# Two convolution-attention blocks on one core: the begin rebuilt, batch norm and block 1's weights prepared later

## The reference

```python
x = x + L0(gn(x)); x = x + L1(gn(x))

def L0(f):                      # linear attention, 8 heads of 16
    x = chan_ln(f, g_norm)      # over channels, at each position
    q, k, v = (depthwise3x3(w1 @ x, dw) for each of the three)
    q = softmax(q, channels of a head) * 16**-0.5;  k = softmax(k, positions)
    ctx = k v^T  per head;  out = silu(q ctx)
    return chan_ln(out_w @ out, g_out)

def L1(x):                      # ReLU linear attention, heads of 8
    qkv = w_qkv @ x
    y = grouped1x1(depthwise5x5(qkv, w_dw), w_pw)
    m = concat(qkv, y); q, k = relu, relu; v gets a row of ones
    out = (v k^T) q, divided by its last row
    return batchnorm(w_proj @ out)   # with given mean and variance
```

## Time and profile before

| | us |
|---|---|
| median of 3 runs (314.0 to 317.98) | 317.24 |
| the profiled execution | 313.73 |
| its span, first to last instruction | 312.0 |
| busy in it: PE, DVE, ACT, POOL | 252.5, 196.5, 150.9, 109.8 |

### The profile page before, as it was taken

How to read it: one execution, slowest core, us unless ns; L and a number is a source line. 1 busy time by engine, 2 the same in 40 slices (tenths; PEclk the granted TensorE clock), 3 DMA queues, 4 the chain that set the end, 5 groups by cost and what they waited for, 6 DMA issues and landing times. The chain is left out here.

```text
span 312.0 us, 13310 instructions
## 1 busy us (share of the span) xinstructions
PE 252.5 (81%) x5715; PEld 190.7 (61%) x5715; DVE 196.5 (63%) x640; ACT 150.9 (48%) x364; POOL 109.8 (35%) x311
## 2 busy tenths in 40 slices
PE   0347799739889599975789979978999989889995
PEld 0235577517568477764566757766877767567761
DVE  3788887408987457999697875654324233457674
ACT  0457575318983467665453537531433347522220
POOL 8035555006866417763341314111112111253200
PEclk9999799959999999999599999999999999999999
DMA  7720078990001200000008281753000000002112
GB/s 235 123 47 3 0 171 211 213 218 9 4 4 24 45 3 2 2 2 0 3 2 184 44 183 41 169 143 65 4 4 4 4 4 4 2 4 69 69 47 91
DMA packets 15499, 19.18 MB, mean 61 GB/s; under 512 B 3904, under 2 KB 9024, under 8 KB 15440
## 3 DMA queue, kind: packets, MB, share of 16 engines
q1 hardware_dynamic: 11936, 17.15, 22.8%
q10 hardware_dynamic: 3504, 1.18, 2.2%
HBM read 3.54 MB, written 2.20 MB: 18 GB/s over the span
## 5 line engine op out<-in xcount | busy, mean ns | idle before, releaser
L1092 PE MATMUL bank<-cin,tband 64*32 64x240 f32 (+2 forms) x3072 | 84.9, 368 | 12.3 <-DMA cin<-cin 5.8
L1092 PEld LDWEIGHTS bank<-cin,tband 64*32 64x32 f32 x3072 | 65.4, 107 | 30.7 <-issue 15.7
L906 DVE STREAM_TRANSPOSE cpos<-bank 128x256 f32<-128x256 f32 x96 | 36.3, 422 | 51.1 <-PE bank L1092 50.9
L568 ACT ACTIVATE tband<-tband,row_edge 128x96 f32<-128x96 f32 (+1 forms) x96 | 32.3, 393 | 39.1 <-POOL tband L417 38.3
L1088 PE MATMUL bank<-ident,rings 128*128 128x128 f32 x192 | 32.2, 297 | 18.5 <-ACT rings L520 7.5
L1088 PEld LDWEIGHTS bank<-ident,rings 128*128 128x128 f32 x192 | 22.7, 150 | 32.4 <-ACT rings L520 9.9
L858 DVE STREAM_TRANSPOSE cin<-bank 128x768 f32<-128x768 f32 x32 | 31.0, 975 | 8.0 <-PE bank L1092 8.0
L453 POOL TENSOR_SCALAR ring_v<-cpos,mask_b 128x512 f32<-128x512 f32 x30 | 20.8, 707 | 36.2 <-PE bank L1092 20.4
L520 ACT ACTIVATE rings<-bank,ln_b,ln_s 128x128 f32<-128x128 f32 x64 | 24.1, 463 | 13.7 <-POOL ln_b L405 13.3
L417 POOL TENSOR_TENSOR tband<-taps,pw 128x160 f32<-128x160 f32 x24 | 11.0, 460 | 44.2 <-PE bank L1092 44.2
L1092 PE MATMUL bank<-w0t,rings 128*32 128x192 f32 x512 | 24.2, 345 | 2.7 <-DVE cin L858 2.0
(11 more groups left out here) (131 smaller groups left out, 421.0 us busy)
## 6 DMA issues: line engine op xcount, KB each, us to landing
cin<-cin SPq DMA_DIRECT2D x48, 192.0 KB, 4.3
cin<-cin SPq DMA_DIRECT2D x20, 128.0 KB, 3.9
xin<-in_x_dram SPq DMA_DIRECT2D x4, 512.0 KB, 6.0
out_dram<-rings SPq DMA_DIRECT2D x16, 128.0 KB, 1.8
cin<-cin ACTq DMA_DIRECT2D x4, 128.0 KB, 4.1
taps<-tap_rows SPq DMA_DIRECT2D x16, 30.0 KB
taps<-tap_rows SPq DMA_DIRECT2D x16, 18.0 KB
rings<-in_L_conv_w_qkv_dram ACTq DMA_DIRECT2D x1, 192.0 KB, 6.9
```

The costliest lines, as they stand in the source:

```text
L568: last = a.activation(dst[:, :, 1 + e], dst[:, :, 0], ACT.Copy, scale=row_edge[:, e:e + 1])
L906: last = v.transpose(cpos[n % NS // TS][:, :, :, g * CG:(g + 1) * CG], bank[2 * (n % 4) + q][:, 0:B * HH])
L1092: return t_.matmul(dst, stationary, moving, start=start, stop=stop, skip_group_check=True)
```

## The change

- Loads: x in five loads of 2, 2, 4, 4 and 4 images; w_qkv, w_proj, w_pw and the five vectors are issued by SP behind x, no longer by ACT.
- The turning of the taps moves from DVE to POOL, behind its masks.
- The small masks move to the very begin of DVE. The first group norm is made in three lots (images 0 to 3, 4 to 7, 8 to 15) in place of two of eight; reading the sums (`gn_read`, with a semaphore `s_gnr`) is apart from scaling.
- PE puts the weight transposes of block 0 between the two products of the first lot.
- `fold_batchnorm` moves behind `conv_out(17)` in the convolution of block 0.
- Block 1's weights: PE's products move behind step 1 of the attention loop (bank 7 in place of 4), and the copies out go from ACT to DVE at step 2.
- SP waits for the first chunk's four transfers before it issues those of the other two, in both blocks.
- In block 1 PE waits for the read sums only, and the last lot's scale is made behind `attn_div`.

```diff
+GN0 = ((0, 4), (4, 8), (8, 16))
+X_LOADS = ((0, 2), (2, 4), (4, 8), (8, 12), (12, 16))
+FOLD_AT = 17
...
+            for (b0, b1), done in zip(X_LOADS, s_x):
+                sp.dma_start(xin[:, b0 * NPOS:b1 * NPOS].rearrange("p (b n) -> p b n", n=NPOS),
+                             x[b0:b1].rearrange("b c h w -> c b (h w)")).then_inc(done, 16)
+            sp.dma_start(staging[:, 4 * C:7 * C].rearrange("p (t c) -> p t c", t=3),
+                          w_qkv.rearrange("(t p) c -> p t c", t=3)).then_inc(s_w, 16)
+            sp.dma_start(wproj, w_proj).then_inc(s_w, 16)
...
                 for r in range(2):
                     both_odd_quads(sp, 0, r, 0)
+                sp.wait_ge(s_db[0], 16 * 4 * (b + 1))
                 for c in range(1, NC):
...
+            def tap_rows():
+
+                pool.wait_ge(s_dw, 16 * 4)
...
+                for h in range(2):
+                    last = g.tensor_copy(rows[:, h, :, :, 0:K0], src[:, h, :, :, ::-1])
...
                 if step + 1 < PAIRS:
-                    if step + 1 == PAIRS // 2:
-                        act.wait_ge(s_gn, 2)
+                    for c in (1, 2):
+                        if step + 1 == GN0[c][0] // 2:
+                            act.wait_ge(s_gn, c + 1)
                     xg(step + 1)
...
             def tanh(i):
+                if i == 0:
+                    act.wait_ge(s_wt, 2)
...
-            def gn_scale(c, b0, n, ps, work=None):
+            def gn_read(c, n, ps):
                 dve.wait_ge(s_gnp, 2 * c + 2)
-                link(v.tensor_copy(gtmp[:, 2, 0:n], ps[:, B:B + n]))
+                v.tensor_copy(gtmp[:, 2, 0:n], ps[:, B:B + n]).then_inc(s_gnr, 1)
+
+            def gn_scale(c, b0, n, work=None):
+                dve.wait_ge(s_gnr, c + 1)
...
-            link(x_stats(0, B // 2))
-            gn_aggregate(0, 0, B // 2)
-            gn_variance(0, 0, B // 2, bank[7])
-            gn_scale(0, 0, B // 2, bank[7])
+            dve.wait_ge(s_ident, 1)
+            small_masks()
+            link(x_stats(0, 4))
+            gn_aggregate(0, 0, 4)
+            x_stats(4, 6)
+            gn_variance(0, 0, 4, bank[7])
+            link(x_stats(6, 8))
+            gn_read(0, 4, bank[7])
+            gn_scale(0, 0, 4)
...
-            tap_rows()
+            gn_aggregate(1, 4, 4)
+            x_stats(8, 9)
...
                 if step == 0:
-                    link(x_stats(B // 2, B))
-                    gn_aggregate(1, B // 2, B // 2)
+                    gn_variance(1, 4, 4, bank[7])
                 if step == 1:
-                    gn_variance(1, B // 2, B // 2, bank[7])
+                    gn_read(1, 4, bank[7])
+                    gn_scale(1, 4, 4)
+                    link(x_stats(9, 16))
+                    gn_aggregate(2, 8, 8)
                 if step == 2:
-                    gn_scale(1, B // 2, B // 2, bank[7])
-                    dve.wait_ge(s_ident, 1)
-                    small_masks()
-                    fold_batchnorm()
+                    gn_variance(2, 8, 8, bank[7])
+                    gn_read(2, 8, bank[7])
+                    gn_scale(2, 8, 8)
...
                 conv_out(n)
+                if n == FOLD_AT:
+                    fold_batchnorm()
...
+            def block1_weights_out():
+
+                dve.wait_ge(s_wt, 2)
+                v.tensor_copy(w1t[:, :].rearrange("p (t h e) -> p h t e", t=3, e=HD1),
+                              bank[7][:, 0:3 * C].rearrange("p (h t e) -> p h t e", t=3, e=HD1))
...
                     ctx_mask(step - 2)
+                if step == 2:
+                    block1_weights_out()
...
+                if step == at + 1:
+                    gn_scale(5, 2 * i0, 2 * (i1 - i0))
...
-            for k in range(2):
-                gn_mean(0, k, 0, B // 2, bank[7])
-
+            gn_mean(0, 0, 0, 4, bank[7])
             pe.wait_ge(s_ident, 1)
             pe.wait_ge(s_w0, 16 * 5)
             for n in range(4):
                 last = t_.transpose(tile(bank[0], n), wst[n], ident[:, :])
             last.then_inc(s_wt, 1)
+            gn_mean(0, 1, 0, 4, bank[7])
...
+                if step < 2:
+                    gn_mean(1, step, 4, 4, bank[7])
                 if step == 2:
-                    gn_mean(1, 1, B // 2, B // 2, bank[7])
...
+                    for k in range(2):
+                        gn_mean(2, k, 8, 8, bank[7])
+
+            def block1_weights():
+                pe.wait_ge(s_bnw, 1)
+                pe.wait_ge(s_w, 16 * 8)
+                pe.wait_ge(s_ce, NS)
...
+                if step == 1:
+                    block1_weights()
...
                 if n == 0:
-                    pe.wait_ge(s_gn, 5)
+                    pe.wait_ge(s_gnr, 6)
```

More of the change, by code:

```diff
@@ L160, in conv_blocks_kernel @@
         gn_sums = bank[0], bank[4], bank[7]
-        s_x = [sem(f"x_quarter{n}_loaded") for n in range(4)]
+        s_x = [sem(f"x_from_image{b0}_loaded") for b0, _ in X_LOADS]
         s_w0 = sem("block0_weights_loaded")
@@ L384, in _ @@
             block_diagonal(mask8, HD1).then_inc(s_const, 1)
+            def tap_rows():
+                pool.wait_ge(s_dw, 16 * 4)
+                rows = zrow0[:, PAD:PAD + NG * K0 * PITCH].rearrange("c (g s k n) -> c g s k n", g=2, s=NS, k=K0)
+                src = dwst0.rearrange("c (s g k n) -> c g s k n", s=NS, g=2, k=K0)
+                for h in range(2):
+                    last = g.tensor_copy(rows[:, h, :, :, 0:K0], src[:, h, :, :, ::-1])
+                last.then_inc(s_z0, 1)
+                rows = zrow1[:, PAD:PAD + NG * K1 * PITCH].rearrange("c (g t s k n) -> c g t s k n", g=2, t=3, s=TS,
+                                                                    k=K1)
+                src = dwst1.rearrange("c (s g t k n) -> c g t s k n", s=TS, g=2, t=3, k=K1)
+                for h in range(2):
+                    for t in range(3):
+                        last = g.tensor_copy(rows[:, h, t, :, :, 0:K1], src[:, h, t, :, :, ::-1])
+                last.then_inc(s_z1, 1)
+            tap_rows()
             def layernorm(n):
@@ L574, in _ @@
             last_odd_quads(0)
[L575 to L578, removed]
-                   bank[4][:, 0:3 * C].rearrange("p (s g t e) -> p g s t e", g=2, t=3, e=HD1)[:, :, :, 0])
-            for g in range(2):
-                a.copy(pw[half(g), :, :].rearrange("p (t s) o -> p t s o", t=3),
-                       bank[5][half(g), 0:3 * C].rearrange("p (s g t o) -> p g t s o", s=TS, g=2, t=3)[:, g])
-            a.copy(wpt[:, :, :].rearrange("p t c -> p (t c)"), bank[6][:, 0:2 * C]).then_inc(s_wte, 1)
             def residual(i):
@@ L638, in xg1 @@
             def xg1(i):
-                act.wait_ge(s_gn, 3 + [i < i1 for i0, i1, _ in GN1].index(True))
+                act.wait_ge(s_gn, 4 + [i < i1 for i0, i1, _ in GN1].index(True))
                 act.wait_ge(s_kt, PAIRS) if i < 2 else act.wait_ge(s_qkv, 2 * (PAIRS + i - 1))
@@ L863, in x_stats @@
                 for b in range(b0, b1):
-                    if b % 4 == 0:
-                        dve.wait_ge(s_x[b // 4], 16)
+                    for (first, _), done in zip(X_LOADS, s_x):
+                        if b == first:
+                            dve.wait_ge(done, 16)
                     last = v.bn_stats(gstats[:, b, :], xin[:, b * NPOS:(b + 1) * NPOS])
                 return last
-            link(x_stats(0, B // 2))
-            gn_aggregate(0, 0, B // 2)
-            gn_variance(0, 0, B // 2, bank[7])
-            gn_scale(0, 0, B // 2, bank[7])
+            dve.wait_ge(s_ident, 1)
[7 more added lines that the diff above has]
+            gn_scale(0, 0, 4)
             dve.wait_ge(s_gn, 1)
@@ L1242, in project @@
             def project(i):
+                if i == 0:
+                    pe.wait_ge(s_wte, 2)
                 pe.wait_ge(s_sl, i + 1)
```

79 lines of the change are left out of this document (28 added, 51 removed).

## The result

The changed kernel took 317.49 us (median of 20 runs, 315.61 to 321.6) beside 316.32 us for the kernel before on the same chip (20 runs, 312.94 to 319.48). The two medians are 1.2 us apart; the ratio, here and in all experiments, compares the fast runs alone, since a kernel's slow runs lie more than 1.5% above its fastest. It is 1.0112, with a 95% interval of 1.008 to 1.0144: 1.1% slower, some 3.5 us, and less than the 2% named in the prediction. The forecast difference was +1.6 us. The profiled execution took 318.22 us, its span 316.5, 4.5 us longer than the span of before. So the size of the loss is known only as 1.2 to 4.5 us, by how it is taken; what follows compares two single executions.

The account below looks back on a forecast made before the run. The prediction saw stages following one another, delays in DVE-fed chains kept to the end, and the begin bounded by the second pair's product. Terms 0 - 0.5 + 2.0 + 0.5 - 0.4 = +1.6 on 317.24 gave 318.8 us, range 312.5 to 321.5.

Parts of the forecast that it names:

- Begin: Start to end of second pair's product: 38.0 against 38.01, so 0 (ends -1.5 and +1.6).
- eight of them at 0.38 in place of 0.2: +1.4: First lot: POOL's tap copies slow some eight small DVE operations, +1.4 us (0 to 2), gn_b at 14.7.
- 31.1 + 1.42 + 0.5 + 1.38: Begin: third lot out, then ACT's images, copy and layer norm output, reaching 34.4; second pair's product ends at 38.0.
- rival 3: Begin: ACT's in-order work makes it slower if the third lot comes after about 31.5; +4.0, 321.2 us; chance 0.12.
- First transfers: Convolution start: SP holds eight transfers until the first four have landed; -0.5 us (0.3 to -2.0).
- Fold behind set 17: Block 0's convolution: fold waits for POOL's product, first k maximum later than 103.86; +2.0 us (0.35 to 2.3).
- the last part of the prediction: Signs expected in the profile after, among them a fold of about 5 us from set 17, one operation ending with POOL's.
- six more sets at 0.715: After the fold ends at 101.7, six depthwise sets at 0.715 us each bring the first k maximum to 106.0.
- Weights: Attention: five DVE copies of block 1's weights take 1.6 us, partly in idle time; +0.5 us (0 to 1.5).
- Read apart: Block 1's statistics: PE freed about 2 us sooner, but DVE's next conversion still waits; -0.4 us (+0.5 to -2.0).
- rivals 1 and 2: No POOL-DVE collision, 315.8 us, chance 0.26; full price for transfers and early read, 0.12; together up to -4.4, 312.8 us.

Follow-up runs that it names:

- twelfth kernel: Old begin with fold ahead of the convolution loop, SP's wait, split read and SP's loads, plus block 1's weights in the attention, against the kernel before: ratio 0.9921, 310.78 us.
- best kernel: Kernel before with fold ahead of the convolution loop, SP's wait, split read and later weights loaded by SP: ratio 0.9801, 306.77 us.

## Why the prediction was right, and where its steps failed

That no difference of 2% would show was right, and 317.49 is 1.3 under the forecast time. The closeness of that time is partly luck: it was built on a median of three runs, 317.24, and the twenty runs give 316.32 for the same kernel. The sum was +1.6 where the ratio gives 3.5, the medians 1.2 and the two traces 4.5, and several of its terms were wrong, in both directions.

- **Begin: 0 forecast, +1.1 found.** The first half held. The read was forecast at 10.9 and stood at 11.02, held by g_norm (issued at 2.87, landed 6.6 us later at 9.5, so no earlier than the 9.2 of before) and PE's transposes. The step "eight of them at 0.38 in place of 0.2: +1.4" failed: the taps landed at 13.5, not at 11, so POOL's copies met no chain, and each gn_b came 1.3 earlier than forecast (13.36, 21.49, 29.77). What failed against this was the way to the second pair's product, "31.1 + 1.42 + 0.5 + 1.38": it left out that ACT's copy (33.67) waits for PE's transposes behind the first pair's products. These started 2.96 late, behind the third pair's images on ACT and the third lot's turn over PE, and took 4.89, most of them at the duration of half clock. The second pair's product in turn was spared its idle of 1.99 and ran at full clock (2.81 for 4.05), so that its end, 39.11 against 38.01, is only 1.1 late. Half of rival 3 had happened, and not by its condition, since the third lot was out before 31.5. The run with the first lot unblocked and the one with two lots show both parts. I also took the begin as one sum; the old begin without the fold gains 2 to 3 us by itself (60.51 to 58.46 and 57.32), and the rebuilt one loses that.
- **First transfers: -0.5.** The row says -0.48. The run without the wait does not bear it out by itself.
- **Fold behind set 17: +2.0 forecast, +4.1 found.** The first copy waited for POOL's product as said, 1.99 us to about 100.25 against 100.16, and the fold took 5.2, as the last part of the prediction named. What failed is "six more sets at 0.715": PE does not run beside the fold. It had filled its banks, idled 2.66, and then did sets 22 and 23 in 4.28 us, three times the 0.715 a set, at a granted clock of 0.53 and 0.62 in the two windows from 104 to 108. The product left out gave back 2.1 of the 4.1, the fold elsewhere all of what can be measured.
- **Weights: +0.5 forecast, +0.7 found**, from the steps of 4.17 and 3.47 between second and third maximum. The mechanism was right. The twelfth kernel puts the price in another setting at 3.8 us by the two ratios, with the half clock in it.
- **Read apart: -0.4 forecast, -1.16 found.** I took it that DVE's next conversion would wait for the scale all the same. It didn't: the first denominator came 2.17 sooner (6.65 against 8.82), and only 1.01 was given back at the next, where ACT waited 4.62 for gn_b (row 190.42 of ACT).
- **Not foreseen:** the clock's return, +1.05, and 0.78 less in block 1's convolution. Most of the latter is PE's own issue: the idle times that the trace puts down to it after 215 us add up to 3.3 before and 2.7 after.

One sum has a slip: rivals 1 and 2 together give -1.4 - 2.0 + 0.35 + 0.5 - 2.0 = -4.55, not -4.4, which moves the lower end by 0.15.

## What to carry to other kernels

Cutting a first lot smaller pays only if nothing else gates the read of it, and each further lot puts a whole turn over three engines in front of products that were due; follow the products, not the first lot. A block of small operations belongs into an idle stretch of its engine: the same fold cost 0 there, some 2 us where it filled an engine that PE leans on, and 4 where a long operation of POOL shut it out as well. When moving work out of a begin, first look at what the begin gains by that alone.

## What the runs showed of the hardware

- **The granted clock comes back at another point in each kernel.** In the earlier trace rows it falls under the first transfers. The second output of the convolution came 1.14 to 1.43 behind the first in three kernels (clock back 1.8 to 3.1 us after the first set) and 1.98 to 2.36 in the others (4.2 to 5.7 us), with no tie found to any one edit; the kernel with masks first had its first set 0.89 earlier than the best kernel and its first k maximum 0.83 later, and 1.21 of these 1.72 us lie between its first two outputs (2.35 against 1.14). The Trainium skill (TensorE: Matmul & The Clock Gate, "What's actually happening") calls the number of slow products run-variable. With one trace for each kernel the traces can't show that, but the mean granted clock of the twenty runs of the changed kernel alone lay between 0.957 and 0.978. So a difference of 1 us between two single profiles can't be put down to an edit before the granted clock in both has been compared.
- **A fall can follow a stall.** After 2.66 us of idle the clock was at 0.53; in the kernel with the fold in the same place but POOL's product left out, PE idled 0.43 and no fall followed. That the stall brings the fall is not shown. In five kernels with the fold ahead of the loop the clock fell too between 102 and 112 us; PE's longest idle time there was the 1.84 us it waits for ACT between the first two k maxima, and the kernel before has the same 1.84 without a fall.
- **A small operation of DVE can last as long as the one of POOL beside it.** Besides the cases above, DVE's small masks at the begin of the changed kernel took 1.21 (a copy) and 1.04 us (128x2) in place of 0.28 and 0.17 and ended at 3.84, with POOL's memset from 2.69 to 3.76. It cost nothing, as x's first images came later, at 4.15.
- **PE waits for its own issue** in block 1's convolution, 0.15 to 0.60 us at a time. The two timelines, before:

```profile
249.43 3.44 PE L1092 MATMUL bank<-cin,tband 64*32 64x240 f32 x127 [0.40 <-issue]
253.37 3.42 PE L1092 MATMUL bank<-cin,tband 64*32 64x224 f32 x127 [0.50 <-issue]
```

and after:

```profile
236.62 3.44 PE L1119 MATMUL bank<-cin,tband 64*32 64x240 f32 x127 [0.40 <-issue]
240.55 10.10 PE L1119 MATMUL bank<-cin,tband 64*32 64x224 f32 x382 [0.49 <-issue]
```

Most come behind 127 or 128 matmul instructions or about a multiple of that (382 is 3 x 127 and one), some are missing, and their sum behind 215 us was between 1.1 and 3.8 in the fourteen traces. Each matmul has a weight load of its own in the profile, so 127 or 128 of them are about 255 instructions of PE. What supplies the instructions was not looked into.
- **A small load can land late.** The last tap load was issued by 5.3 and its data was there only at 13.5; what holds it was not tried.
